# All other products of a causal attention kernel issued to TensorE as strips of 32 weight columns

## What is computed

```python
x = x + 0.5 * ffn(layernorm(x), W, b, V_r, C)      # base + low-rank correction: z @ (W.T + V_r @ C.T) + b
x = x + attention(layernorm(x), W_attn, W_proj)
x = x + 0.5 * ffn(layernorm(x), W, b, V_r, C)
...
# attention, 16 heads of 16 features, causal
att = einsum('bhid,bhjd->bhij', q, k) / sqrt(16)
att = where(causal, att, -inf)
att = polymax(att)          # (x**2 + 1) / 1000 for x > 0; (1 - x/100) / 1000 for -100 <= x <= 0; else 0
y = einsum('bhij,bhjd->bhid', att, v)
return y @ W_proj
```

## Time and profile before

| | |
|---|---|
| median of 3 runs | 2059.39 us |
| profiled execution, its own time | 2050.64 us |
| its span, first to last instruction | 2048.9 us |
| mean granted TensorE clock | 0.974 of full |
| TensorE matmuls, busy | 1752.2 us, 86%, 12694 of them |
| TensorE weight loads, busy (beside the matmuls) | 759.3 us, 37% |
| VectorE, busy | 1259.6 us, 61% |
| ScalarE, busy | 1340.1 us, 65% |
| GpSimd, busy | 1324.9 us, 65% |

### The profile page before, as it was taken

How to read it: one execution, slowest core, us unless ns; L and a number is a source line. 1 busy time by engine, 2 the same in 40 slices (tenths; PEclk the granted TensorE clock), 3 DMA queues, 4 the chain that set the end, 5 groups by cost and what they waited for, 6 DMA issues and landing times.

```text
span 2048.9 us, 35693 instructions
## 1 busy us (share of the span) xinstructions
PE 1752.2 (86%) x12694; PEld 759.3 (37%) x12694; DVE 1259.6 (61%) x2065; ACT 1340.1 (65%) x1634; POOL 1324.9 (65%) x1419
## 2 busy tenths in 40 slices
PE   5678789898989899898989989898998899998875
PEld 3544334242433334343433434343333333333334
DVE  2455676666666666666566666666565666676652
ACT  1244567776777676677667667766777777777551
POOL 3354557686767767677676767767666767676652
PEclk9899999999999999999999999999999999999997
DMA  2343331323323142332324233231423222223111
GB/s 81 112 147 111 112 118 54 111 76 93 94 79 112 54 131 69 100 101 89 109 57 128 71 99 103 88 109 48 131 64 96 73 76 67 75 64 91 55 34 55
DMA packets 155062, 181.15 MB, mean 88 GB/s; under 512 B 22012, under 2 KB 129660, under 8 KB 152836
## 3 DMA queue, kind: packets, MB, share of 16 engines
q1 hardware_dynamic: 154884, 178.82, 29.6%
HBM read 102.43 MB, written 76.30 MB: 87 GB/s over the span
## 4 chain that ended last, share of the span: by engine, by line
PE 64%; DVE 14%; issue 9%; ACT 9%; POOL 2%; DMA 2%; SPq 0%; DVEq 0%; ACTq 0%; POOLq 0%
PE y_ps L974 25%; PE score L974 19%; PE bank L974 17%; DVE rp L909 7%; ACT rp L818 2%; PE bank L993 2%; ACT rp L838 2%; ACT rp L834 2%; DVE lin L915 2%; POOL z L685 1%; DVE bnst_ln L934 1%; DMA part_scratch<-parts 1%; DVE qk_max L921 1%; DVE rest L454 1%; ACT lin L824 1%
## 5 line engine op out<-in xcount | busy, mean ns | idle before, releaser
L909 DVE TENSOR_SCALAR rp<-score 128x1024 f32<-128x1024 f32 (+2 forms) x864 | 860.8, 1002 | 359.8 <-PE score L974 354.6
L723 POOL TENSOR_TENSOR rp<-rp 128x1024 f32<-128x1024 f32 (+1 forms) x416 | 756.6, 1828 | 191.6 <-DVE rp L909 180.2
L974 PE MATMUL score<-qs,ks 96*128 96x512 bf16 (+3 forms) x2560 | 673.0, 351 | 197.3 <-DVE rp L909 105.0
L818 ACT ACTIVATE rp<-score 128x1024 f32<-128x1024 f32 (+1 forms) x416 | 413.3, 993 | 409.7 <-PE score L974 408.4
L974 PE MATMUL y_ps<-rp,vt 128*16 128x512 f32 (+3 forms) x5120 | 598.7, 540 | 6.8 <-ACT rp L838 4.9
L834 ACT ACTIVATE rp<-rp,rise 128x1024 f32<-128x1024 f32 (+1 forms) x416 | 455.6, 1118 | 1.3 <-POOL rp L698 1.3
L974 PEld LDWEIGHTS score<-qs,ks 96*128 96x128 bf16 x2560 | 204.7, 98 | 583.8 <-DVE rp L909 277.9
L698 POOL TENSOR_SCALAR_AFFINE_SELECT rp<-rp 128x256 f32<-128x256 f32 (+1 forms) x384 | 184.0, 481 | 362.2 <-ACT rp L818 191.5
L838 ACT ACTIVATE rp<-rp 128x1024 f32<-128x1024 f32 (+2 forms) x224 | 290.6, 1297 | 121.9 <-DVE rp L909 73.2
L974 PE MATMUL bank<-w_ffn,zT 128*128 128x256 f32 x512 | 168.6, 427 | 7.7 <-ACT zT L779 7.7
L974 PEld LDWEIGHTS y_ps<-rp,vt 128*16 128x16 f32 x5120 | 84.1, 94 | 230.3 <-issue 171.7
(11 more groups left out here) (78 smaller groups left out, 1350.8 us busy)
## 6 DMA issues: line engine op xcount, KB each, us to landing
part_scratch<-parts SPq DMA_DIRECT2D x16, 1536.0 KB, 7.5
qs<-part_scratch SPq DMA_DIRECT2D x384, 64.0 KB
ks<-part_scratch SPq DMA_DIRECT2D x384, 64.0 KB, 2.3
state_scratch<-st_new SPq DMA_DIRECT2D x16, 528.0 KB
st<-state_scratch SPq DMA_DIRECT2D x64, 132.0 KB
x_sb<-in_L_attn_x_dram SPq DMA_DIRECT2D x16, 512.0 KB, 4.4
x_scratch<-x SPq DMA_DIRECT2D x16, 512.0 KB, 5.4
qT_scratch<-qkT SPq DMA_DIRECT2D x16, 512.0 KB, 3.7
```

Source lines behind the costliest of these rows:

```text
L723: pool.tensor_tensor(half, half, half, ALU.mult).then_inc(squared["pool"], 1)
L818: nc.scalar.activation(rp[T % RP_BUFS][:, 2:4, off:CH], score[H % S_BUFS][:, :, off:CH], ACT.Relu).then_inc(raised["act"], 1)
L909: nc.vector.tensor_scalar(rp[T % RP_BUFS][:, 2 * u:2 * u + 2, off:CH], score[H % S_BUFS][:, :, off:CH], 0.0, RISE, ALU.max, ALU.add).then_ ...
L974: return nc.tensor.matmul(*args, start=start, stop=stop, skip_group_check=True)
```

## The change

A helper, strips, cuts the weights of a product into slices of at most 32 columns and issues one matmul for each, which writes the slice of output partitions that belongs to these columns. All of them stream the same moving operand. It takes the place of mm in five places: feed-forward, output and projection products (128 columns, so 4 strips), qT (4), state (66 columns, so 3 strips, of 32, 32 and 2), the scores (4), and the product of states and qT (4). The products with the values are as they were, and so are transposes. The semaphore of a product is signalled by its last strip.

```diff
--- before.py
+++ after.py
@@ -973,6 +973,13 @@
             def mm(*args, start=True, stop=True):
                 return nc.tensor.matmul(*args, start=start, stop=stop, skip_group_check=True)
 
+            def strips(dst, w, src, start=True, stop=True):
+
+                for j in range(0, w.shape[-1], STRIP):
+                    part = slice(j, min(j + STRIP, w.shape[-1]))
+                    ins = mm(dst[part], w[:, part], src, start=start, stop=stop)
+                return ins
+
             pe.wait_ge(const_ready, CONSTS)
             pe.wait_ge(w_loaded, 16 * 6)
             for k in range(KC):
@@ -1014,11 +1021,11 @@
                     w = {"ffn": w_ffn, "out": w_ffn, "proj": w_out, "v": w_qkv[:, :, 2 * DM:], "k": w_qkv[:, :, DM:2 * DM]}[kind]
                     src = {"ffn": zT, "out": z3T, "proj": y_c, "v": z2T, "k": z2T}[kind]
                     blk = 2 * i + piece // 2
-                    ins = mm(half, src[:, kc, P * blk:P * blk + P], w[:, kc, :], start=kc == 0, stop=kc == KC - 1)
+                    ins = strips(half, src[:, kc, P * blk:P * blk + P], w[:, kc, :], start=kc == 0, stop=kc == KC - 1)
                 if kind == "qT":
                     if first:
                         wait_emptied(pe, "z2T", a, 1)
-                    ins = mm(dst[:], w_qkv[:, kc, P * i:P * i + P], z2T[:, kc, :], start=kc == 0, stop=kc == KC - 1)
+                    ins = strips(dst[:], w_qkv[:, kc, P * i:P * i + P], z2T[:, kc, :], start=kc == 0, stop=kc == KC - 1)
                 if kind == "kT":
                     if first:
                         wait_emptied(pe, "k", a, 1)
@@ -1028,7 +1035,8 @@
                     if first:
                         wait_emptied(pe, "v", a, 1)
                     for g in range(QUADS):
-                        ins = mm(dst[0:QR, QD * g:QD * (g + 1)], k_sb[:, i, g // 2, QD * (g % 2):QD * (g % 2) + QR], v_sb[:, g, i, :])
+                        ins = strips(dst[0:QR, QD * g:QD * (g + 1)], k_sb[:, i, g // 2, QD * (g % 2):QD * (g % 2) + QR],
+                                     v_sb[:, g, i, :])
                 if piece == PIECES[kind] - 1:
                     ins.then_inc(job_done, 1)
 
@@ -1046,8 +1054,8 @@
                         wait_lin(pe, H - S_BUFS)
                 for v in range(2):
                     head = 2 * u + v
-                    ins = mm(score[H % S_BUFS][:, v, off:CH], ks[:, head, P * kb:P * kb + P],
-                             qs[:, head, CH * c + off:CH * c + CH])
+                    ins = strips(score[H % S_BUFS][:, v, off:CH], ks[:, head, P * kb:P * kb + P],
+                                 qs[:, head, CH * c + off:CH * c + CH])
                 ins.then_inc(qk_done, 1)
 
             def values(T):
@@ -1059,8 +1067,8 @@
                     if w >= 2:
                         pe.wait_ge(y_copied, w - 1)
                     for m in range(NB):
-                        mm(y[:, P * m:P * m + P], st[:, NB * c + m, :], qT[:, CH * c + P * m:CH * c + P * m + P],
-                           start=m == 0, stop=False)
+                        strips(y[:, P * m:P * m + P], st[:, NB * c + m, :], qT[:, CH * c + P * m:CH * c + P * m + P],
+                               start=m == 0, stop=False)
                 if t in DIAG:
                     wait_lin(pe, 2 * T)
                     wait_lin(pe, 2 * T + 1)
```

## The result

The changed kernel took 1989.5 us as the median of five runs (1981.72 to 1993.33), against 2057.55 (five as well, 2052.87 to 2062.42) before: a ratio of 0.9668, 95% interval 0.9642 to 0.9694, 68 us less. The forecast was 1955 us, 1900 to 2040. The direction held and the time is in the range, but the gain is 68 us where 96 were forecast. The profiled execution took 1981.7 us.

The account below looks back on a forecast made before the run. The prediction took TensorE's stream, emptied at weight-width changes, to bound about four fifths of a round. 172 - 28 - 24 = 120 us less TensorE time, times 0.8 = 96, from 2050.6 gave 1955 us, range 1900 to 2040.

Parts of the forecast that it names:

- What bounds the kernel: About four fifths of round time follow TensorE, which loses 0.10 us entering and 0.12 leaving narrow weights (128 to 16 columns).
- the turnarounds removed: Around 640 values groups, turns worth 141 us go, plus 31 us behind float32 jobs: 172 us of TensorE time.
- Turnarounds added: 128 groups of transposes keep 128 columns between strips and now pay 0.22 us each: 28 us more TensorE time.
- The strips' own pace: At 27 ns a strip, short score products cost 14 us more and states 10: 24 us more TensorE time.
- the slower rival: On TensorE, issue, weight loads or code fetch set a least time per strip; at 62.5 ns, 2227 us; chance 0.08.
- From TensorE to the end: Of 120 us less TensorE time, four fifths reach the end: 96 us off the profiled 2050.6, giving 1955 us.
- Mostly absorbed: TensorE runs ahead but waits for score buffers; only 35% of 120 us arrives, 42 us: 2009 us; chance 0.16.
- Bound by issue: Strips on TensorE meet a least time each; at 62.5 ns they cost 364 us extra: 2227 us; chance 0.08.
- The turns stay: Something other than width empties the array between score and values; nothing goes, short strips cost 24 us: 2070 us; chance 0.05.

Follow-up runs that it names:

- scores alone: The changed kernel with strips kept only for the scores; jobs, states and st with qT whole again: 2130 us, 1.035 of the kernel before.
- all but scores: The changed kernel with whole score products; jobs, states and st with qT stay strips: 2085 us, 1.0135 of the kernel before.
- slices of 64: The changed kernel with weight slices of 64 columns in place of 32, values still 16 columns: 2164 us, 1.0516 of the kernel before.

## Why the prediction was right, and where its size was off

*What bounds the kernel, and the turnarounds removed.* Right, and at the size given: 0.10 going in, 0.12 coming out and 0.11 behind a float32 job all went. That this last 0.11 was a weight load which could not be done ahead is the prediction's reading; the rows show its size, not its cause. That it is the width that counts is shown by three kernels: scores alone and all but scores both turn more often and are slower, and slices of 64 turn against those of 16. Neither the kind of data nor the rows do it: in the change bfloat16 scores of 96 rows, float32 jobs of 128 and st with qT of 66 follow each other without a turn. The Trainium skill, page "TensorEngine Tiling (Array Packing)", section Key Properties, states that changing the tiling mode, not just the tile, drains TensorE. The rows agree, in the run with slices of 64 columns too. The 0.10 to 0.14 us is from the rows.

*Turnarounds added.* Right: 0.11 ahead of the transposes and 0.14 with them, for 0.10 and 0.12.

*The strips' own pace.* Wrong by a small term: 24 us were charged and nothing was due. The shortest score halves run at 15 ns a strip, not 27, and a state piece of 24 strips takes 0.44 us (below) where the whole one took 0.50, a gain of some 4 us over 64 pieces. 27 ns was what lin's two float32 passes take in the array, not a floor of issue. So by the count TensorE should save 172 - 28 + 4 = 148 us, not 120, and the slower rival, issue at 46 ns a strip or more, is refuted by the same rows. The loss of the fast weight load, which the prediction weighed, shows no price in the timeline: a shortest score half takes 0.12 us in strips.

148 is a count, not a measurement. The traces can be asked for the saving itself. I took every distance from the first start of a group to the first start of the next and subtracted the smooth price of its columns (0.215 us for 512 in bfloat16 or 256 in float32, a quarter of it for a strip). Where the clock was full and no wait followed, what is left over sums to 181 us before and 49 after, 132 less, and the states' columns are 7 us cheaper as three strips of four: 139 us.

*From TensorE to the end.* This is the term that was off. "By the chain four fifths of a round follow it: 0.8 x 120 = 96 us" should have been near one half: 68 us is 0.57 of the predicted 120, 0.49 of the 139 and 0.46 of the 148. That the gain was forecast as well as it was is in part luck, for the TensorE term was too small and the factor too large. Another 7 us of the distance between 1955 and 1989.5 come from the start of the sum: the profiled execution, 2050.6 us, was faster than the median of 2057.55. The same sums over the two traces say where the difference went. Of 139 us, 12 are paid back at the lower clock. 17 more stand in the ends of products just before a wait: these ends are modelled, and the next product no longer runs over them, for the scores now wait for VectorE 231 times, not 192. That leaves the 110 us by which TensorE's busy time fell. 42 more are idle time of TensorE, 38 of them the longer waits of the scores for VectorE. 139 - 12 - 17 - 42 = 68, against a span that is 69 us shorter. So where the missing part stands is accounted for; why VectorE comes late is not. Its wait for the square root and its double halves were each tried, and neither explains it alone.

The chain's share was a poor guide. The chain of the kernel before has 0.80 of a round on TensorE and issue, and 117 us added to it cost 0.76 of themselves, but the change, which takes the turns away from the same kernel, gave 0.49. Around the changed kernel the factor is 0.56 for 117 us added and 0.60 for 110 us removed, although the chain of the last lies on TensorE for 40% only. So around the changed kernel added and removed work count about alike; what sank is the factor between the kernel before and the change. Products added at every first half and turns removed around the values are also not the same work, and no run separates the two reasons.

*The rivals.* "Mostly absorbed" had the mechanism that took the missing part, waits for the score buffers, at 0.35 of 120 for its price; the gain of 68 us lies midway between its 42 and the 96 of the forecast, and the full round of 115.9 us is nearer to its 117 than to 113. "Bound by issue" is refuted by the strips at 15 ns. "The turns stay" is refuted by the timeline.

## What to carry to other kernels

Where products of few weight columns alternate with wide ones, read start-to-start distances around each kind of neighbour: a surcharge that stands on every change of width is removed by giving all neighbours the same strips, and converting one half of them can be worse than none. Estimate first what the engine's own time loses, and check it in the trace afterwards: here a count gave 148 us and the distances 139. Don't scale it by the chain's share. Of work taken away a good deal less may arrive, since the next wait is met sooner. A dummy product more measures the factor for that work in that kernel, not for another change: in the kernel before it gave 0.76, and 0.76 of 148 would have been 112 us, further off than the forecast of 96.

## What was not expected of the hardware

Strips of neighbouring products run into each other. The states use only three of the four strips, the third for 2 columns. I read the rows as the fourth being free for the next score:

```profile
1132.80 0.52 PE L974 MATMUL bank<-v_sb,k_sb 128*32 128x64 f32 x18
1133.10 0.39 PE L974 MATMUL score<-qs,ks 96*32 96x512 bf16 x1
1133.13 0.29 PE L974 MATMUL bank<-v_sb,k_sb 128*32 128x64 f32 x6
1133.24 0.62 PE L974 MATMUL score<-qs,ks 96*32 96x512 bf16 x7
```

The first score strip starts at 1133.10, while six state strips start behind it at 1133.13 and the other seven score strips at 1133.24. Where whole products surround the states, in the trace of before, there is no such overlap.

This matters for the signal. In the second product of the same half the strip that signals the half, the last in the program, starts at 1133.33, ahead of the other three at 1133.46 to 1133.48. In 52 of the 1280 halves it starts over 0.1 us ahead of others of its half. The semaphore is still raised only after all eight: 0.18 us behind the (modelled) end of the signalling strip in these halves, 0.03 us behind the last of its half, and 0.03 us behind its own end elsewhere (medians). So here the signal of the last strip covered the strips issued before it, though starts were not in the order of the program.

Four score strips of 128 columns start within 0.03 us, the next four 0.06 us behind them: 15 ns a strip on average. The page "TensorE: Matmul & The Clock Gate" of the Trainium skill, section "Wait — 56ns, not 53.3ns?", gives about 25 ns as the least distance between starts however short a matmul is; in this trace, over a series of eight strips of four column groups, it is less, and the measurement decides.

VectorE's raising of a score half did not get slower beside operands that are now read four times: 1211 ns median and 1226 at most, against 1212 and 1226 in the earlier trace rows.
